# A recurrence over patches: four additions of shifted rows on VectorE in place of a product with a decay matrix on TensorE, and another order of loads

## What is computed

```python
# layer 1: x = x + _L0_xattn_ref(_layernorm(x), ctx, lens, ...)
h       = rmsnorm(embeds, g_res) @ W_in.T + b_in
h_patch = rmsnorm(ctx, g_init)[..., :512]
s[0] = exp(logp) * h_patch[0];  s[i] = a * s[i-1] + exp(logp) * h_patch[i]   # a: a small constant
depool_out = s[plug]            # a row of s is picked for each of the 512 rows
return depool_out + h
# layer 2: x = x + ffn(_layernorm(x))
xr, xk = (mu * x + (1 - mu) * x_prev for mu in (mu_r, mu_k))
out = sigmoid(xr @ W_r.T) * (square(relu(xk @ W_k.T)) @ W_v.T)
```

## Time and profile before

| | |
|---|---|
| median of 3 runs | 786.76 us (786.43 to 787.09) |
| profiled execution, own time | 788.05 us |
| its span, first to last instruction | 786.5 us |
| PE busy | 756.9 us (96%) |
| DVE busy | 553.8 us (70%) |
| ACT busy | 413.3 us (53%) |
| POOL busy | 173.4 us (22%) |
| mean granted clock of PE | 0.986 of full |

### The profile page before, as it was taken

One profiled execution on the slowest core, in us unless ns is written; L12 is line 12 of the kernel. 1 busy time (PEld: TensorE's weight loads), 2 busy tenths in 40 slices (PEclk: granted clock), 3 DMA queues, 4 the chain that ended last, 5 costly groups with the idle time before them and its releaser, 6 DMA issues.

```text
span 786.5 us, 11081 instructions
## 1 busy us (share of the span) xinstructions
PE 756.9 (96%) x3462; PEld 624.1 (79%) x3463; DVE 553.8 (70%) x1005; ACT 413.3 (53%) x681; POOL 173.4 (22%) x175
## 2 busy tenths in 40 slices
PE   7669899999999999999999999999999999999997
PEld 4457688888888888888888888888888888888876
DVE  4678797685866868586686858667685867667452
ACT  3317755454654645466464546656454665544760
POOL 7244131311213131121313112131311213130000
PEclk9879999999999999999999999999999999999999
DMA  7476153441706244170624417062441706231011
GB/s 256 150 188 166 60 124 132 112 143 47 209 2 167 88 110 144 46 208 0 156 98 109 144 43 211 0 166 88 108 146 41 212 0 160 94 102 20 1 54 54
DMA packets 42765, 85.73 MB, mean 109 GB/s; under 512 B 3536, under 2 KB 3536, under 8 KB 42704
## 3 DMA queue, kind: packets, MB, share of 16 engines
q1 hardware_dynamic: 30624, 63.71, 21.7%
q0 software_dynamic: 9216, 16.78, 13.5%
q10 hardware_dynamic: 2880, 4.76, 1.7%
HBM read 64.26 MB, written 21.76 MB: 109 GB/s over the span
## 4 chain that ended last, share of the span: by engine, by line
PE 85%; DVE 4%; POOL 4%; issue 2%; ACT 2%; DMA 1%; DVEq 0%; POOLq 0%; ACTq 0%
PE bank L484 27%; PE bank L486 27%; PE bank L485 27%; PE bank L588 3%; POOL ring L426 2%; DMA s_rows<-scanned 1%; POOL decay L363 1%; DVE xk_lo L894 1%; DVE scratch L989 0%; DVE ring L1019 0%; DVE gate L1044 0%; ACT scratch L794 0%; POOL rs_a L389 0%; DVE bn_a L923 0%; DVE bn_b L1025 0%
## 5 line engine op out<-in xcount | busy, mean ns | idle before, releaser
L426 POOL DMA_INDIRECT ring<-s_rows,patch_now x60 | 99.4, 1656 | 245.8 <-DMA s_rows<-scanned 214.6
L894 DVE TENSOR_TENSOR xr_lo<-scratch,xr_hi 128x512 fp32r<-128x512 f32 x124 | 85.6, 690 | 68.9 <-ACT xr_hi L704 68.4
L989 DVE SCALAR_TENSOR_TENSOR scratch<-turned,cols,scratch 128x512 f32<-128x512 f32 x128 | 94.6, 749 | 34.4 <-ACT scratch L749 15.0
L484 PE MATMUL bank<-wi_hi,xt_hi 128*128 128x512 f32 x256 | 104.0, 406 | 5.1 <-DVE xt_lo L894 5.1
L704 ACT ACTIVATE turned<-bank 128x512 f32<-128x512 f32 x64 | 33.4, 604 | 143.3 <-PE bank L588 114.7
L484 PE MATMUL bank<-xk_hi,wk_hi 128*128 128x512 f32 x256 | 99.9, 390 | 2.2 <-DVE xk_lo L894 2.2
L485 PE MATMUL bank<-wi_lo,xt_hi 128*128 128x512 f32 x256 | 101.8, 398 | 0.0
L486 PE MATMUL bank<-wi_hi,xt_lo 128*128 128x512 f32 x256 | 101.5, 396 | 0.0
L484 PE MATMUL bank<-wr_hi,xr_hi 128*128 128x512 f32 x256 | 99.7, 389 | 0.8 <-DVE xr_lo L894 0.8
L486 PE MATMUL bank<-xk_hi,wk_lo 128*128 128x512 f32 x256 | 99.6, 389 | 0.0
L485 PE MATMUL bank<-xk_lo,wk_hi 128*128 128x512 f32 x256 | 99.6, 389 | 0.0
(11 more groups left out here) (131 smaller groups left out, 1283.5 us busy)
## 6 DMA issues: line engine op xcount, KB each, us to landing
ring<-in_x SPq DMA_DIRECT2D x16, 1024.0 KB, 7.4
out<-gate SPq DMA_DIRECT2D x64, 256.0 KB
xt<-in_x_turned SPq DMA_DIRECT2D x15, 1024.0 KB, 5.2
ctx_rows<-in_ctx SPq DMA_DIRECT2D x16, 512.0 KB, 8.0
s_rows<-scanned ACTq DMA_DIRECT2D x16, 256.0 KB, 2.0
gate<-in_L_xattn_W_in SPq DMA_DIRECT2D x4, 256.0 KB, 3.4
xt<-in_x_turned SPq DMA_DIRECT2D x2, 512.0 KB, 6.3
turned<-in_L_ffn_W_r SPq DMA_DIRECT2D x1, 1024.0 KB, 7.8
```

The source lines that it names most:

```text
L426: pool.indirect_dma_start(ring[b.slot][:, t, :], None, s_rows[:, :], bass.IndirectOffsetOnAxis(ap=rows, axis=0), compute_op=ALU.add).then_ ...
L484: nc.tensor.matmul(where, lhs_hi, rhs_hi, start=start, stop=False)
L894: return nc.vector.tensor_tensor(to, whole, high, ALU.subtract)
L989: nc.vector.scalar_tensor_tensor(scratch[:, 2 + i % 2, :], turned[:, c, 1:S + 1], cols[:, 1 + which, c:c + 1], scratch[:, i % 2, :], ALU.m ...
```

## The change

For batches 2 to 15 the scan no longer runs on PE. With a decay matrix cut to its first 16 powers, s is built by four doubling steps: with k = 8, 4, 2, 1, each step does `scanned = earlier * a^k + source`, where `earlier` is the source shifted down by k rows (partitions), with zeros in the first k rows, and the source is `u` in the first step and `scanned` after it. A shift across partitions is made by a DMA from SBUF to SBUF that SP issues: 120, 124, 126 and 127 rows of 2 KB. The DVE instruction of a step (`scan_step`) waits for its DMA, and the DMA of the next step waits for it. A fifth DVE instruction (`add_bias`) adds the bias and raises `s_copied`. `clear_head` zeroes 8 rows of `earlier` once per batch. `scan_input` moves up, ahead of `ka_low`; `u_high`, `u_low` and `scan_out` go for these batches. SP's loads come in the order ctx, x, x transposed, with the four shift DMAs behind them and ahead of the stores of the results. Two of the four `add_out` now stand between the third and the fourth step. The "far" branch makes its own `u_hi` and `u_lo`. Batches 0 and 1 keep the product.

The diff's core:

```diff
+def shift_steps(powers):
+    return [(k, powers[k] if k < len(powers) else 0.0) for k in (8, 4, 2, 1)]
...
 @ SP
+            def shift_scan(b):
+                since = b.plus(-2)
+                for n, (k, _) in enumerate(steps_of_scan):
+                    if n == 0:
+                        reached(sp, u_ready, b, 1, 1)
+                    else:
+                        reached(sp, earlier_added, since, STEPS, n)
+                    of = scanned if n else u
+                    sp.dma_start(earlier[k:P, :], of[0:P - k, :]).then_inc(earlier_loaded, 16)
...
+                    reached(sp, far_over, new.plus(-1), 1, 1)
                     rows_added(sp, new.plus(-1))
-                    reached(sp, xt_lo_ready, new.plus(-1), 2, 2)
-                    load_xt(new)
+                    load_ctx(new)
                     reached(sp, out_ready, b.plus(-1), T, T)
...
                     load_x(new)
-                    reached(sp, far_over, new.plus(-1), 1, 1)
-                    load_ctx(new)
+                    reached(sp, xt_lo_ready, new.plus(-1), 2, 2)
+                    load_xt(new)
+                    shift_scan(new)
...
 @ PE
                     if t == SCAN and b.plus(1).exists(B) and not is_first(b):
-                        reached(pe, s_copied, b.plus(1), 1, 1)
                         reached(pe, far_over, b.plus(1), 1, 1)
...
                 if new.exists(B):
-                    scan(new)
                     far(new)
...
 @ ACT
                 elif new.exists(B):
-                    if not is_first(b):
-                        u_high(new)
                     store_scan(new)
...
 @ DVE
+            def scan_step(b, n):
+                since = b.plus(-2)
+                reached(dve, earlier_loaded, since, 16 * STEPS, 16 * (n + 1))
...
+                nc.vector.scalar_tensor_tensor(scanned[:, :], earlier[:, :], steps_of_scan[n][1], (scanned if n else u)[:, :],
+                                               ALU.mult, ALU.add).then_inc(earlier_added, 1)
+            def add_bias(b):
+                reached(dve, earlier_added, b.plus(-2), STEPS, STEPS)
+                nc.vector.tensor_tensor(scanned[:, :], scanned[:, :], bias[:, :], ALU.add).then_inc(s_copied, 1)
```

More of the change, by code:

```diff
@@ L96, in build @@
     powers = decay_powers()
+    steps_of_scan = shift_steps(powers)
+    STEPS = len(steps_of_scan)
+    assert len(powers) <= 2 ** STEPS
     input_gain = math.exp(-EPSILON)
@@ L162, in build @@
         patch_now = sb("patch_now", [P, T], U32)
+        earlier = sb("earlier", [P, D])
         def part(row, start, shape, dt):
@@ L213, in build @@
             "u_ready u_hi_ready u_lo_ready s_done s_copied s_stored patch_picked")
+        head_zeroed, earlier_loaded, earlier_added = sems("head_zeroed earlier_loaded earlier_added")
         dep_added = [sem(f"dep_added{t}") for t in range(T)]
@@ L520, in far @@
                         else:
-                            reached(pe, s_copied, b, 1, 1)
+                            if b.fixed and b.number() < 2:
+                                reached(pe, s_copied, b, 1, 1)
+                            pe.wait_ge(far_u_lo, n[1] * T + 1)
                         product(scan_bank(b)[:, :], decay_hi[:, 1, :], decay_lo[:, 1, :], u_hi[:, :], u_lo[:, :],
                                 True, False).then_inc(far_carried, 1)
-                        pe.wait_ge(far_u_lo, done)
+                        pe.wait_ge(far_u_lo, n[1] * T + c + 1)
                         product(scan_bank(b)[:, :], decay_hi[:, 0, :], decay_lo[:, 0, :], u_hi[:, :], u_lo[:, :],
@@ L945, in scan_input, with clear_head @@
                 reached(dve, rs_c_done, b, 1, 1)
-                reached(dve, u_lo_ready, b.plus(-1), 1, 1)
+                if b.fixed and b.number() < 3:
+                    reached(dve, u_lo_ready, b.plus(-1), 1, 1)
+                else:
+                    reached(dve, earlier_added, b.plus(-3), STEPS, STEPS)
                 nc.vector.scalar_tensor_tensor(u[:, :], ctx_rows[:, 0:D], rs_c[:, :], g_ctx[:, :],
                                                ALU.mult, ALU.mult).then_inc(u_ready, 1)
+            def clear_head(b):
+                reached(dve, earlier_added, b.plus(-2), STEPS, 0)
+                nc.vector.memset(earlier[0:steps_of_scan[0][0], :], 0.0).then_inc(head_zeroed, 1)
+            def scan_step(b, n):
+                since = b.plus(-2)
+                reached(dve, earlier_loaded, since, 16 * STEPS, 16 * (n + 1))
+                if n == 0:
+                    reached(dve, head_zeroed, since, 1, 1)
+                    reached(dve, s_stored, b, 16, 0)
+                    reached(dve, u_ready, b, 1, 1)
+                else:
+                    reached(dve, earlier_added, since, STEPS, n)
+                nc.vector.scalar_tensor_tensor(scanned[:, :], earlier[:, :], steps_of_scan[n][1], (scanned if n else u)[:, :],
[3 more added lines that the diff above has]
+                nc.vector.tensor_tensor(scanned[:, :], scanned[:, :], bias[:, :], ALU.add).then_inc(s_copied, 1)
             def far(b):
@@ L953, in far @@
                 with dve.If(n[0] > 0):
+                    if b.fixed and b.number() < 2:
+                        reached(dve, s_done, b, 1, 1)
+                    nc.vector.tensor_copy(u_hi[:, :], u[:, :]).then_inc(far_u_hi, 1)
+                    dve.wait_ge(far_u_hi, n[1] * T + 1)
+                    low(u_lo[:, :], u[:, :], f32(u_hi[:, :])).then_inc(far_u_lo, 1)
+                    dve.wait_ge(far_u_lo, n[1] * T + 1)
                     for c in range(1, T):
@@ L1084, in iteration @@
                 if is_first(b):
+                    clear_head(new)
                     ka_low(b, 0)
@@ L1092, in iteration @@
                     ka_low(b, 3)
-                    u_low(new)
+                    scan_step(new, 0)
                     norm_b(nxt)
@@ L1096, in iteration @@
                     gating(b, 1)
+                    scan_step(new, 1)
                     x_lo(new, 0)
                     x_lo(new, 1)
-                    scan_out(new)
+                    scan_step(new, 2)
+                    add_out(b, 0)
+                    add_out(b, 1)
+                    scan_step(new, 3)
+                    add_bias(new)
                     far(new)
                     dve.sem_inc(far_over, 1)
-                    add_out(b, 0)
-                    add_out(b, 1)
                     gating(b, 2)
@@ L1113, in iteration @@
                     norm_b(nxt)
+                if new.exists(B):
+                    scan_input(new)
                 for m in range(C):
@@ L1119, in iteration @@
                             x_lo(new, m - 1)
-                        if m == 2:
-                            scan_input(new)
+                        if m in (2, 3):
+                            scan_step(new, m - 2)
                 if is_last(nxt):
                     mixing(nxt, 0, C)
-                if new.exists(B):
-                    u_low(new)
                 if b.exists(B):
@@ L1129, in iteration @@
                 if new.exists(B):
-                    scan_out(new)
+                    scan_step(new, 2)
+                if b.exists(B):
+                    add_out(b, 0)
+                    add_out(b, 1)
+                if new.exists(B):
+                    scan_step(new, 3)
+                    add_bias(new)
                     far(new)
```

2 lines of the change are left out of this document (1 added, 1 removed).

## The result

The changed kernel takes 1030.01 us (median, 1029.43 to 1030.5); the kernel before, measured beside it, 786.6. The ratio is 1.3095, with an interval of 1.3073 to 1.3118. Forecast were 985 us, in a range of 930 to 1040.

The account below looks back on a forecast made before the run. PE, busy for 96% of the span, was taken as the bound. 788.05 - 9.5 (product) + 163.8 (waits, 13 iterations) + 15.0 (iteration 0) + 29.4 (clock) = 986.7, 1.3 less for the median: 985 us, range 930 to 1040.

Parts of the forecast that it names:

- The sharing of rows: Shift DMAs: only as many engines as divide the rows evenly, one for 127 rows, landing in 12.1 us; chance 0.86.
- The round trips: Steps 1 to 3 each wait for a transfer in series: landings of 3.95, 2.1 and 12.1 us, plus 0.25 wake-up each.
- The place of the pause: Between PE's transposes and projection: PE waits 12.6 us for ACT's copy, queued behind the store that follows the bias addition.
- The clock: After each of 14 waits PE restarts at a lower clock, losing 2.1 us each, 29.4 us in all.
- PE's 9.5 us: The scan's three matmuls leave PE: 0.68 us in each of 14 batches, 9.5 us less.
- The loads: The new load order, landing some 4 us later, counted as nothing; at most 4 us per batch if the cover is gone.
- DVE's 36.6 us: DVE's busy time per iteration, rising from 33.4 to about 36.6 of 45.3 us, not becoming the bound.
- The sum per iteration: One loop iteration: 45.3 us, plus PE's wait of 12.6 and the clock loss of 2.1; about 60 us expected.
- Rival 1: Shift transfers spread evenly, rows rounded up: every landing 2.0 us, PE waits 0.35 per batch, 782 us; chance 0.08.
- rival 2: Even spread but slower round trips: from 2.1 us each 0.1 costs 4.2; a 3.0 landing gives 824 us; chance 0.06.

Follow-up runs that it names:

- the table of counts: Round trips by row count, from the changed kernel and one whose shifts move only 117, 122, 125 and 112 rows; the latter took 935.32 us.
- bank_wait: Changed kernel with the wait for the end of the far branch moved from PE's transposes into the branch, which is not entered: 1025.93 us.
- filler17: Changed kernel with 17 plain fp32 matmuls, results unused, added where PE waits in each of 14 iterations: 1004.8 us.
- no_steps: Changed kernel without the four steps and their transfers in batches 2 to 15, the bias being added to `u`: 778.16 us.
- loads_only: Kernel before with only its loads in the changed order (ctx, x, x transposed): 786.72 us.
- parallel_split: Changed kernel with only the shifts by 2 and 1, both from `u` at once, each sent as 112 rows and the rest: 778.4 us.
- split112: Changed kernel with each shift sent as two transfers, 112 rows and the remaining 8, 12, 14 or 15: 827.13 us.

## Why the prediction was right, and where its sizes were off

- **The sharing of rows**, the choice on which all hung, was right: 15, 4, 14 and 1 engines. Shown by the 34 small packets of a batch, by the table of counts and by the split, which gives back 203 us.
- **The round trips were sized too small.** The price of a row was about right (0.085 us; the 112 and the 127 rows alone give 0.086), the fixed part was not: I took 0.25 + 1.3 = 1.55 us from the store of `scanned`, a transfer of 128 rows, and the line needs 2.3. The wake-up was not the cause: SP begins the issue for the 127 rows at 549.12, 0.03 us behind the step. The three round trips were forecast at 18.9 us (4.2 + 2.35 + 12.35) and measured 21.9 (5.66 + 3.14 + 13.08). SP's issue alone takes 0.64 to 0.82 us for these row counts, beside 0.33 for the store; what the rest of the difference is stays open. This is the term that was mis-sized: 3.0 us in 14 batches are 42 of the 45 us between forecast and result. That the range of 930 to 1040 still held the result is in part luck: it was made from the price of a packet and the clock, and allowed nothing for this term.
- **The place of the pause** was right in substance: all hangs on the bias addition. I named ACT's copies as PE's releaser; in the trace it is the wait for the far branch, which holds the projection some 0.5 us longer (1.8 against 1.3 us in bank_wait). I had that wait before me in the code and left it out of the chain. From the end of the addition to the projection I had 1.3 us and it is 1.8, another 7 us in 14 batches.
- **The clock** was forecast at 2.1 us per batch and measured 1.9 (filler17), 3 us less in 14 batches.
- **PE's 9.5 us** were measured at 9.8 (no_steps). **The loads** and DVE's additional work cost nothing where it was tried (loads_only; parallel_split, where DVE is busy for 34.53 us and PE doesn't wait). DVE's 36.6 us were a little too high: 35.77 measured, since `scan_out`, 0.69 us, goes too and I had not taken it off.
- The sum per iteration: 45.3 + 12.6 + 2.1 = 60.0 forecast, 63.2 measured; 3.0 of the 3.2 us are the round trips.
- **Rival 1** needed 2.0 us for a landing and a time of 782. With an even spread (split112) the round trip is 2.8, and the time 827: even then the change would have been slower. That is rival 2: its rule of 4.2 us for each 0.1 us of landing past 2.1 gives, for a landing of 2.8 - 0.25 = 2.55, about 806, too little by 21. The rule's wait is 2.0 us a batch, 28 in all, and PE's pauses at the transposes are 34.7; the rule also has no clock in it, and the mean granted clock is 0.977 against 0.986. The rest was not told apart.

## What to carry to other kernels

A transfer of rows of 2 KB across partitions cost by the rows on its busiest DMA engine, 2.7 us for 7 rows and 13.1 for 127: choose row counts that 16 divides, and send what is left over as a transfer of its own. Steps that pass through a DMA in series took 2.7 to 2.9 us each even when they were shared well; make the shifts independent of each other, from the same source, and issue them early. When an engine that is the bound is relieved, look for the queues in which its next operand stands behind the work that was moved, and cost a pause of PE with its clock added.

## What the runs showed of the hardware that I had not expected

- The issue of a transfer of 124 to 127 rows takes 0.64 to 0.82 us on SP's queue, one of 120 rows 0.88 to 0.99, one of 112 rows 0.52 to 0.58 (split112); the store of 128 rows takes 0.33 on ACT's.
- 64 more matmuls in a loop iteration brought a pause of 3.2 to 3.5 us in every third, where the loop goes back; 17 longer ones, which the trace shows as 34, did not.
- Two waits hang on the same instruction, one through PE's transposes and one through ACT's copies. They hold the projection for times that differ by 0.5 us in the median, so that removing the one that the trace names gave 4 us of 243.
